# Issuing four key blocks first, reordering the tail of cross-attention, and making half of three layer norms one stage earlier

## The chip, the cores and the metric

The kernel runs on one core of one Trainium2 chip. The metric is device time in microseconds (us) of that core; lower is better. The engines are TensorE (PE, its weight loads PEld), VectorE (DVE), ScalarE (ACT), GpSimd (POOL) and SyncE (SP), which issues most of the DMAs. Each engine works through its own instructions in order and waits only on semaphores.

## The reference

The input x has 8 batches of 128 rows of 128 numbers, and a context of 8 x 77 rows of 96. Two decoder layers are computed, each of three sublayers that add to x. All four norms taken ahead of a sublayer subtract a row's mean and divide by its deviation:

```
layer 0: x += attention(norm(x))          16 heads of 64, with a relative position bias
         x += cross_attention(norm(x), context)   16 heads of 8, 77 keys
         x += mixture(norm(x))            16 experts, 8 chosen by sigmoid scores, and a shared one
layer 1: x  = strided attention block(norm(x)), with its own post-norms and a feed-forward part
         x += cross_attention(norm(x), context)
         x += mixture(norm(x))            8 experts of width 512, 2 chosen, with a capacity limit
```

## The kernel before

The kernel is one program in stages, each a block that all engines enter and leave together: setup (with norm 0), `attention0`, cross-attention of layer 0 (called x0 below), `mixture0`, `layer_norm("n3_")` (norm 2), `attention1`, cross-attention of layer 1 (x1), `mixture1`, store. Row vectors live on the 128 partitions, batches side by side: `x_all` and `xn_all` are [128, 8, 128], and `xnT_all` is the transposed copy that the matmuls read.

A norm of all eight batches (`norm_vector`, `norm_gpsimd`, `norm_tensor`, `norm_scalar`) is: on DVE four `bn_stats`, four `bn_aggr` and one add of epsilon (L173, L176, L178) for batches 0 to 3, the same for 4 to 7, then eight `tensor_scalar` (L181) that write the normed rows; on POOL one power for each half (L188); on PE eight transposes (L193); on ACT one copy for each half (L198). Norm 1 stands at the beginning of x0, norm 2 in a block of its own between `mixture0` and `attention1`, norm 3 at the beginning of x1. Norms ahead of the two mixtures are made inside cross-attention, batch by batch (L1021 to L1072).

**Cross-attention** (`cross_attention(l, ...)`) begins with its norm. Then PE makes the queries of batches 0 and 1 for all head groups (L821), ACT and DVE split them into a high and a low part (L923, L980), and the queries of batches 2 to 7 (L826, L935, L988) are brought to their place by DMA: SP issues 12 copies for part j = 0 (batches 2, 3) and 12 for part 1 (L807). The keys of a batch are one DMA of 462 KB into one of four buffers (L797). Before, SP issues the keys of batches 0 and 1, then part 0 of the queries, then keys of batches 2 and 3, then part 1, then in x1 six loads for the next stage, and then the keys of batches 4 to 7. The main loop has 16 steps n (two for each batch) of a software pipeline: scores of step n (PE L867), clamp and maximum (DVE L1008 and L1025; in x1 L1011 and L1029), subtraction (POOL L1063 in x0), exponential (ACT L968), transposes (PE L901), copy (ACT L963), values (PE L891), and for each batch the turn back (PE L911), the division (DVE L1040, L1044), transposes (PE L874), the output product (PE L857), the addition to x (DVE L1016), and the norm for the mixture: statistics on DVE, power and rows on POOL (L1068, L1071), transpose (PE L880), copy (ACT L946), router logits (PE L1145 or L1805). Steps 16 to 24 drain this pipeline. Within one step DVE adds to x first (batch (n-7)/2) and divides last (batch (n-5)/2). PE waits in step 4 for part 0 of the queries and the keys of batch 2, in step 8 for part 1 and the keys of batch 4.

**mixture0** has 34 units u: the shared expert on both halves of the rows, then experts 0 to 15 on the first half (u = 2 to 17), then on the second (u = 18 to 33). In step u PE makes gate(u) and up(u) (L1209 to L1211), and down(u-3). ACT takes the silu (L1287), POOL multiplies by the routing weight (`e_gc`, L1304), DVE multiplies by up (`e_h`, L1342), ACT copies the high part (L1266), DVE subtracts (`e_h_lo`, L1348). After step 22 the first half is turned back on PE (L1243) and DVE adds it to x (L1354) after its unit 22.

## Time and profile before

| | us |
|---|---|
| median of 3 runs | 558.77 |
| lowest, highest | 557.69, 562.34 |
| the profiled execution, its own time | 559.68 |
| its span in the trace | 557.9 |
| PE, DVE, ACT, POOL busy | 474.1, 371.1, 332.8, 267.3 |

The span is the time from the first to the last instruction of the profiled execution; its own time is 1.78 longer. Busy shares are means over stages with different limits, so for a change that touches stage borders the timeline around each border has to be read: which instruction starts late, and what released it. PEclk is TensorE's granted clock as a share of 2.4 GHz; 0.50 is 1.2 GHz.

### The profile page before, as it was taken

To read this page: it belongs to the slowest core of one execution; us is meant where nothing else is said; L and a number is where in the kernel's file an instruction comes from. 1 tells how busy PE (TensorE), PEld (TensorE's weight loads), DVE (VectorE), ACT (ScalarE), POOL (GpSimd) and SP (SyncE) were. 2 spreads that over 40 slices of the span, in tenths; PEclk is the share of its full clock that TensorE was granted. 3 is DMA by queue.
4 is the path that set the end of the run, shared out by engine and by line. 5 is a ranking of instruction groups with operands and counts; after the bars stand their busy time and mean duration, and the time that the engine had idled before them with its cause. 6 is when DMAs were issued, how large, how long until landed. Compare 5 with 4: busy or idle time off the path is not lost. (4 is left out here: it accounts for less than half of the span.)

```text
span 557.9 us, 9954 instructions
## 1 busy us (share of the span) xinstructions
PE 474.1 (85%) x3161; PEld 359.8 (64%) x3161; DVE 371.1 (67%) x911; ACT 332.8 (60%) x655; POOL 267.3 (48%) x294
## 2 busy tenths in 40 slices
PE   4689999999578877899994999656689779999995
PEld 3577888876356655688882578444466556777774
DVE  4787777774646745566665476767357454999995
ACT  3687777775446763356552465224467555988883
POOL 1699879777434642466662750113072231745420
PEclk9799999999779995899997899796789969999999
DMA  6614342425255000444332200003580002111101
GB/s 184 210 43 120 101 120 72 126 79 133 71 140 147 1 2 1 136 133 132 116 93 69 58 0 1 0 1 78 139 218 1 2 2 75 33 45 38 38 0 38
DMA packets 34688, 41.80 MB, mean 75 GB/s; under 512 B 5178, under 2 KB 26612, under 8 KB 34420
## 3 DMA queue, kind: packets, MB, share of 16 engines
q1 hardware_dynamic: 33796, 40.65, 26.2%
q10 hardware_dynamic: 848, 0.60, 0.4%
q8 instruction: 23, 0.38, 0.3%
q14 instruction: 21, 0.17, 0.1%
HBM read 30.70 MB, written 8.18 MB: 70 GB/s over the span
## 5 line engine op out<-in xcount | busy, mean ns | idle before, releaser
L1304 POOL TENSOR_TENSOR e_gc<-e_g,e_c 128x512 f32<-128x512 f32 x32 | 41.8, 1309 | 38.1 <-ACT e_g L1287 23.1
L2090 DVE TENSOR_TENSOR e_h_lo<-e_h,e_h_hi 128x512 fp32r<-128x512 f32 x56 | 55.6, 1045 | 3.4 <-ACT e_h_hi L1968 3.4
L1780 POOL TENSOR_TENSOR m_w_hi<-m_w,m_one 128x512 fp32r<-128x512 f32 x16 | 19.7, 1232 | 68.1 <-DMA m_w<-in_L_ffn_W 30.4
L963 ACT ACTIVATE x_pT<-x_turn 77x1024 f32<-77x1024 f32 x32 | 32.7, 1021 | 32.3 <-PE x_turn L901 32.3
L1964 ACT ACTIVATE e_h<-e_h,m_b 128x512 f32<-128x512 f32 x64 | 43.8, 691 | 8.3 <-PE e_h L1864 8.3
L557 ACT ACTIVATE a_p<-xn_all,a_least 128x128 f32<-128x128 f32 x128 | 40.7, 390 | 6.1 <-DVE a_least L596 6.0
L1266 ACT ACTIVATE e_h_hi<-e_h 128x512 fp32r<-128x512 f32 x34 | 21.5, 632 | 33.8 <-DVE e_h L1342 23.9
L901 PE MATMUL x_turn<-consts,x_p 128*77 128x128 f32 x256 | 38.3, 296 | 3.9 <-ACT x_p L968 3.9
L1348 DVE TENSOR_TENSOR e_h_lo<-e_h,e_h_hi 128x512 fp32r<-128x512 f32 x34 | 23.7, 698 | 26.5 <-ACT e_h_hi L1266 26.5
L703 POOL TENSOR_TENSOR a_p<-a_p,a_r 128x512 f32<-128x512 f32 x32 | 33.3, 1042 | 15.0 <-DVE a_r L605 15.0
L901 PEld LDWEIGHTS x_turn<-consts,x_p 128*77 128x77 f32 x256 | 30.3, 158 | 13.4 <-ACT x_p L968 11.1
L593 DVE TENSOR_TENSOR xn_all<-a_score,w_bias 128x256 f32<-128x256 f32 x64 | 24.1, 418 | 18.6 <-PE a_score L446 18.6
L1968 ACT ACTIVATE e_h_hi<-e_h 128x512 fp32r<-128x512 f32 x56 | 33.9, 636 | 0.0
L1063 POOL TENSOR_TENSOR x_s<-x_s,x_m 128x616 f32<-128x616 f32 x16 | 19.5, 1217 | 27.7 <-DVE x_m L1025 27.7
L891 PE MATMUL x_pv<-x_pT,vx 77*9 77x128 f32 x512 | 22.5, 299 | 9.6 <-ACT x_pT L963 9.6
L547 ACT ACTIVATE a_pT<-a_turn 128x512 f32<-128x512 f32 x32 | 19.0, 593 | 19.4 <-PE a_turn L456 19.4
L1862 PE MATMUL e_h<-m_x_hi,m_w_hi 128*128 128x512 f32 x64 | 26.4, 412 | 0.0
L1011 DVE TENSOR_REDUCE x_m<-x_score 128x8 f32<-128x616 f32 x16 | 12.7, 794 | 20.3 <-PE x_score L867 20.2
L867 PE MATMUL x_score<-x_ks,x_qs 96*128 96x308 f32 x64 | 19.2, 386 | 7.7 <-DMA x_ks<-kstack 6.4
L1864 PE MATMUL e_h<-m_x_hi,m_w_lo 128*128 128x512 f32 x64 | 25.6, 400 | 0.0
L1863 PE MATMUL e_h<-m_x_lo,m_w_hi 128*128 128x512 f32 x64 | 25.6, 400 | 0.0
L1862 PE MATMUL e_y<-e_h_hi,m_w_hi 128*128 128x512 f32 x56 | 24.9, 444 | 0.4 <-DVE e_h_lo L2090 0.4
(300 smaller groups left out, 1448.2 us busy)
## 6 DMA issues: line engine op xcount, KB each, us to landing
e_c<-spread SPq DMA_DIRECT2D x32, 256.0 KB, 3.3
x_ks<-kstack SPq DMA_DIRECT2D x16, 462.0 KB, 5.5
kstack<-a_blk_hi SPq DMA_DIRECT2D x32, 154.0 KB, 3.1
m_w<-in_L_ffn_W SPq DMA_DIRECT2D x16, 256.0 KB, 3.1
a_raw<-in_experts SPq DMA_DIRECT2D x17, 192.0 KB, 2.5
kstack<-a_blk_lo SPq DMA_DIRECT2D x16, 154.0 KB, 2.9
su_reversed<-scratch SPq DMA_DIRECT2D x1, 1024.0 KB, 5.6
w_wkv<-in_L_attn_Wkv SPq DMA_DIRECT2D x1, 1024.0 KB, 7.6
```

The source lines that it names most:

```text
L557: act.activation(p[n % 4][:, h, :], s[n % 2][:, h, :], ACT.Exp, bias=least[:, n % 4, h:h + 1]).then_inc(S["exp_done"], 1)
L593: dve.tensor_tensor(s[n % 2][:, own_heads, :], score[half][:, 0:2, :], bias0[:, NG * hg + half:NG * hg + NG:2, :], ALU.add).then_inc(S["bi ...
L703: pool.tensor_tensor(p[n % 4][:, :, :], p[n % 4][:, :, :], free(r[:, n % 4, :], [[1, NG], [0, P]]), ALU.mult).then_inc(S["normed"], 1)
L901: mm = pe.transpose(tb[0:NKV, u, P * j:P * j + P], p[k % 2][:, u, j, :], ident)
L963: act.activation(pT[k % 2][:, :, :], tb[0:NKV, :, :], ACT.Copy).then_inc(S["turned_out"], 1)
L1304: pool.tensor_tensor(gc[k % 2][:, :], g[u % 2][:, :], c[k % NC][:, :], ALU.mult).then_inc(S["weighted"], 1)
L1862: pe.matmul(out, w_hi, hi, start=start, stop=False)
L1863: pe.matmul(out, w_hi, lo, start=False, stop=False)
L1864: return pe.matmul(out, w_lo, hi, start=False, stop=stop)
L1964: act.activation(h[half][f], hb[f][:, :], ACT.Gelu, bias=b1[j][:, f:f + 1]).then_inc(S["gelu_done"], 1)
L1968: act.activation(h_hi[half][f - 1][:, :], h[half][f - 1], ACT.Copy).then_inc(S["hi_done"], 1)
L2090: dve.tensor_tensor(h_lo[half][f][:, :], h[half][f], h_hi[half][f][:, :].bitcast(F32), ALU.subtract).then_inc(S["lo_done"], 1)
```

## The change

`norm_vector` and `norm_gpsimd` are cut into functions for one half h: `norm_stats`, `norm_rows`, `norm_power`. Then:

- Norm 1, batches 0 to 3: statistics in `attention0` after DVE's step n = G = 32, the power after POOL's last step, the rows after DVE's step 35. x0 keeps batches 4 to 7.
- Norm 2, batches 0 to 3: in `mixture0`, statistics after DVE's unit 23, power after POOL's unit 24, rows after DVE's unit 25, four transposes after PE's step 27 (into the bank `rb`), ACT's copy after its step 28. The later turn of the second half waits for that copy.
- Norm 3, batches 0 to 3: statistics between the two halves of the last norm in `attention1`, the power on POOL after its third; the rows are the first work of DVE in x1.
- Cross-attention, both layers: SP issues the keys of batches 0 to 3 first. In the drain (n > 16) DVE divides before it adds to x; the rows of batch 7 are written by DVE instead of POOL; the router logits are issued in steps 17, 19, 21, 23 and 24 instead of 18, 20, 22 and 24.

The setup block calls the same functions in the same order as before.

```diff
-    def norm_vector(dve, n):
-
-        for h in range(2):
-            half = slice(HB * h, HB * h + HB)
-            for b in range(HB * h, HB * h + HB):
-                dve.bn_stats(stats[:, b, :], x_all[:, b, :]).then_inc(stats_done, 1)
-            for b in range(HB * h, HB * h + HB):
-                dve.wait_ge(stats_done, B * n + b + 1)
-                dve.bn_aggr(mv[:, b, :], stats[:, b, :]).then_inc(mv_done, 1)
-            dve.wait_ge(mv_done, (B + 2) * n + (HB + 1) * h + HB)
-            dve.tensor_scalar(var[:, half], mv[:, half, 1], LN_EPS, None, ALU.add).then_inc(mv_done, 1)
-        for b in range(B):
-            dve.wait_ge(rstd_done, 2 * n + b // HB + 1)
+    def norm_stats(dve, n, h):
+        half = slice(HB * h, HB * h + HB)
+        for b in range(HB * h, HB * h + HB):
+            dve.bn_stats(stats[:, b, :], x_all[:, b, :]).then_inc(stats_done, 1)
+        for b in range(HB * h, HB * h + HB):
+            dve.wait_ge(stats_done, B * n + b + 1)
+            dve.bn_aggr(mv[:, b, :], stats[:, b, :]).then_inc(mv_done, 1)
+        dve.wait_ge(mv_done, (B + 2) * n + (HB + 1) * h + HB)
+        dve.tensor_scalar(var[:, half], mv[:, half, 1], LN_EPS, None, ALU.add).then_inc(mv_done, 1)
+
+    def norm_rows(dve, n, h):
+        dve.wait_ge(rstd_done, 2 * n + h + 1)
+        for b in range(HB * h, HB * h + HB):
             dve.tensor_scalar(xn_all[:, b, :], x_all[:, b, :], mv[:, b, 0:1], rstd[:, b:b + 1],
                               ALU.subtract, ALU.mult).then_inc(normed, 1)
 
-    def norm_gpsimd(pool, n):
-        for h in range(2):
-            half = slice(HB * h, HB * h + HB)
-            pool.wait_ge(mv_done, (B + 2) * n + (HB + 1) * (h + 1))
-            pool.tensor_tensor(rstd[:, half], var[:, half], eps_pow[:, half], ALU.pow).then_inc(rstd_done, 1)
+    def norm_power(pool, n, h):
+        half = slice(HB * h, HB * h + HB)
+        pool.wait_ge(mv_done, (B + 2) * n + (HB + 1) * (h + 1))
+        pool.tensor_tensor(rstd[:, half], var[:, half], eps_pow[:, half], ALU.pow).then_inc(rstd_done, 1)
...
-                norm_vector(dve, n)
+                norm_stats(dve, n, 1)
+                norm_rows(dve, n, 1)
 
             @block.gpsimd
             def _(pool):
-                norm_gpsimd(pool, n)
+                norm_power(pool, n, 1)
 
             @block.tensor
             def _(pe):
-                norm_tensor(pe, n, turned)
+                norm_tensor(pe, n, turned, half=1)
 
             @block.scalar
             def _(act):
-                norm_scalar(act, n, turned)
+                norm_scalar(act, n, turned, half=1)
...
+                    if n == G:
+                        dve.wait_ge(S["x_out"], 2)
+                        norm_stats(dve, 1, 0)
+                    if n == G + 3:
+                        norm_rows(dve, 1, 0)
...
+                norm_power(pool, 1, 0)
...
-                keys(0)
-                keys(1)
+                for b in range(KEYS):
+                    keys(b)
...
-                    if j == 0:
-                        for b in range(2, KEYS):
-                            keys(b)
...
-                    if ahead is not None and n >= STEPS + 2 and n % 2 == 0:
-                        for b in range(0 if n == STEPS + 2 else n // 2 - 5, n // 2 - 4):
+                    if ahead is not None and (n > STEPS and n % 2 == 1 or n == 2 * SLOTS + 4):
+                        for b in {STEPS + 1: (0, 1), STEPS + 3: (2, 3, 4), 2 * SLOTS + 4: (7,)}.get(n, (n // 2 - 5,)):
                             pe.wait_ge(S["xT_out"], since["xT_out"] + b + 1)
                             ahead.logits(pe, b, tb)
...
-                norm_vector(dve, norm)
+                if l == 1:
+                    norm_rows(dve, norm, 0)
+                norm_stats(dve, norm, 1)
+                norm_rows(dve, norm, 1)
...
+                def finish(b):
+                    dve.wait_ge(S["back_done"], since["back_done"] + b + 1)
+                    dve.reciprocal(r[:, :], back[:, :, DH]).then_inc(S["recip_done"], 1)
+                    dve.wait_ge(S["recip_done"], since["recip_done"] + b + 1)
+                    if b >= 2:
+                        dve.wait_ge(S["slot_done"], since["slot_done"] + b - 1)
+                    dve.tensor_tensor(o[b % 2][:, :].rearrange("p (h d) -> p h d", d=DH), back[:, :, 0:DH],
+                                      free(r[:, 0:1], [[1, H], [0, DH]]), ALU.mult).then_inc(S["normed"], 1)
...
+                    if n > STEPS and batch_at(n, 5) is not None:
+                        finish(batch_at(n, 5))
...
+                    if b == B - 1:
+                        dve.wait_ge(S["rstd_done"], since["rstd_done"] + B)
+                        dve.tensor_scalar(xn_all[:, b, :], x_all[:, b, :], mv[:, b, 0:1], rstd[:, b:b + 1],
+                                          ALU.subtract, ALU.mult).then_inc(S["xn_done"], 1)
+                    if n < STEPS and batch_at(n, 5) is not None:
+                        finish(batch_at(n, 5))
...
-                norm_gpsimd(pool, norm)
+                norm_power(pool, norm, 1)
...
+                    if b is not None and b < B - 1:
...
+    NEXT = 2
...
+    ADDED = LAST_OF[0] + LAG + 2
...
-                    pe.wait_ge(S["added"], 1)
+                    pe.wait_ge(copied, 2 * NEXT + 1)
...
+                if u == ADDED + 5:
+                    norm_tensor(pe, NEXT, [rb[:, :]], half=0)
...
+                if u == ADDED + 6:
+                    norm_scalar(act, NEXT, [rb[:, :]], half=0)
...
+                if u == ADDED + 2:
+                    norm_power(pool, NEXT, 0)
...
+                if u == ADDED + 1:
+                    dve.wait_ge(S["added"], 1)
+                    norm_stats(dve, NEXT, 0)
+                if u == ADDED + 3:
+                    norm_rows(dve, NEXT, 0)
...
+                    if k == 2:
+                        norm_power(pool, 3, 0)
...
+                    if h == 0:
+                        dve.wait_ge(S["x_ready"], HB)
+                        norm_stats(dve, 3, 0)
```

## Rows read from the trace of the kernel before

**Rows 1.** Windows: PE, PEld, DVE, ACT, POOL busy (instructions), clock, DMA share, GB/s.

```profile
140.90:215.80 74.90, 56.29 (x516) 40.89 (x516) 42.59 (x115) 42.43 (x68) 34.96 (x35) 0.83 0.26 67
216.50:298.60 82.10, 77.31 (x318) 60.99 (x318) 49.97 (x106) 43.19 (x74) 41.85 (x32) 0.95 0.34 104
```

**Rows 2.** Timeline, beginning of x0: start, us, engine line, tiles, [idle before <-releaser].

```profile
140.94 1.28 ACT L920 ACT_TABLE_LOAD   x1 [1.24 <-PEq L327]
...
140.97 0.87 DVE L173 BATCH_NORM_STATS2 stats<-x_all 128x6 f32<-128x128 f32 x4 [0.32 <-PEq L327]
...
142.40 1.02 POOL L188 TENSOR_TENSOR rstd<-var,eps_pow 128x4 f32<-128x4 f32 x1 [5.27 <-DVE var L178]
...
143.49 2.36 DVE L181 TENSOR_SCALAR xn_all<-x_all,mv,rstd 128x128 f32<-128x128 f32 x8
...
145.16 0.60 ACT L198 ACTIVATE xnT_all<-x_turn 128x512 f32<-128x512 f32 x1 [2.93 <-PE x_turn L193]
```

**Rows 3.** Window over attention0's last 8 us, columns as in rows 1.

```profile
132.20:140.20 8.00, 6.95 (x49) 4.42 (x47) 1.27 (x3) 2.23 (x5) 4.77 (x6) 1.00 0.34 80
```

**Rows 4.** Timeline, DVE in the last microseconds of attention1.

```profile
371.14 0.69 DVE L1729 TENSOR_TENSOR a_y<-b_pv,xn_all 128x512 f32<-128x512 f32 x1 [2.73 <-PE b_pv L1556]
```

**Rows 5.** Timeline, beginning of x1.

```profile
376.04 0.87 DVE L173 BATCH_NORM_STATS2 stats<-x_all 128x6 f32<-128x128 f32 x4 [0.32 <-PEq L1440]
...
380.24 0.60 ACT L198 ACTIVATE xnT_all<-x_turn 128x512 f32<-128x512 f32 x1 [2.94 <-PE x_turn L193]
...
382.60 0.48 DVE L980 SCALAR_TENSOR_TENSOR x_qs<-x_score,cols,x_qs 32x256 fp32r<-32x256 f32 x1 [1.68 <-ACT x_qs L923]
```

**Rows 6.** Timeline, keys issued by SP and the score products that waited for them.

```profile
159.16 1.05 SPq L797 DMA_DIRECT2D x_ks<-kstack  x2
...
163.63 0.85 PE L867 MATMUL x_score<-x_ks,x_qs 96*128 96x308 f32 x2 [0.70 <-DMA x_ks<-kstack]
...
395.12 1.05 SPq L797 DMA_DIRECT2D x_ks<-kstack  x2
...
399.48 0.85 PE L867 MATMUL x_score<-x_ks,x_qs 96*128 96x308 f32 x2 [3.96 <-DMA x_ks<-kstack]
...
413.94 0.52 PE L867 MATMUL x_score<-x_ks,x_qs 96*128 96x308 f32 x2 [1.72 <-DMA x_ks<-kstack]
```

**Rows 7.** Timeline, the drain of x0.

```profile
205.98 0.63 PE L911 MATMUL x_back<-consts,x_oS 128*128 128x128 f32 x4 [0.78 <-ACT xnT_all L946]
...
208.47 0.25 DVE L1040 RECIPROCAL x_r<-x_back 128x16 f32<-128x16 f32 x1
...
213.36 0.80 POOL L1071 TENSOR_SCALAR xn_all<-x_all,mv,rstd 128x128 f32<-128x128 f32 x1
...
214.31 0.45 PE L880 MATMUL x_back<-consts,xn_all 128*128 128x128 f32 x1 [1.17 <-POOL xn_all L1071]
```

**Rows 8.** Timeline, mixture0's loop: DVE's units 24 and 25, PE's step 28.

```profile
276.42 0.68 DVE L1342 TENSOR_TENSOR e_h<-e_up,e_gc 128x512 f32<-128x512 f32 x1
...
278.41 0.68 DVE L1342 TENSOR_TENSOR e_h<-e_up,e_gc 128x512 f32<-128x512 f32 x1
...
279.79 0.69 DVE L1348 TENSOR_TENSOR e_h_lo<-e_h,e_h_hi 128x512 fp32r<-128x512 f32 x1 [0.70 <-ACT e_h_hi L1266]
...
280.70 0.40 PE L1209 MATMUL e_gate<-e_x_hi,we_hi 128*128 128x512 f32 x1
```

**Rows 9.** Timeline of POOL, mixture0's loop: the product in two places.

```profile
234.48 1.47 POOL L1304 TENSOR_TENSOR e_gc<-e_g,e_c 128x512 f32<-128x512 f32 x1 [0.23 <-ACT e_g L1287]
...
276.34 1.33 POOL L1304 TENSOR_TENSOR e_gc<-e_g,e_c 128x512 f32<-128x512 f32 x1 [1.17 <-ACT e_g L1287]
```

**Rows 10.** Windows in mixture0 and x0, columns as in rows 1.

```profile
160.00:170.00 10.00, 9.30 (x74) 6.76 (x75) 3.57 (x5) 4.58 (x7) 2.43 (x2) 0.50 0.84 200
...
225.00:227.00 2.00, 0.00 (x0) 0.00 (x0) 1.79 (x15) 0.00 (x0) 0.00 (x0) 1.00 0.09 25
228.00:231.00 3.00, 3.00 (x8) 2.35 (x8) 0.43 (x1) 0.00 (x0) 1.84 (x2) 0.50 0.81 282
```

More of the change, by code:

```diff
@@ L307, in _ @@
                 dve.wait_ge(ld_x, 16)
-                norm_vector(dve, 0)
+                for h in range(2):
+                    norm_stats(dve, 0, h)
+                for h in range(2):
+                    norm_rows(dve, 0, h)
                 dve.wait_ge(ld_bias, 16)
@@ L315, in _ @@
                 pool.wait_ge(eps_set, 1)
-                norm_gpsimd(pool, 0)
+                for h in range(2):
+                    norm_power(pool, 0, h)
         return mine
@@ L1036, in _ @@
                                           ALU.add).then_inc(S["var_done"], 1)
-                    b = batch_at(n, 5)
-                    if b is not None:
-                        dve.wait_ge(S["back_done"], since["back_done"] + b + 1)
-                        dve.reciprocal(r[:, :], back[:, :, DH]).then_inc(S["recip_done"], 1)
-                        dve.wait_ge(S["recip_done"], since["recip_done"] + b + 1)
-                        if b >= 2:
-                            dve.wait_ge(S["slot_done"], since["slot_done"] + b - 1)
-                        dve.tensor_tensor(o[b % 2][:, :].rearrange("p (h d) -> p h d", d=DH), back[:, :, 0:DH],
-                                          free(r[:, 0:1], [[1, H], [0, DH]]), ALU.mult).then_inc(S["normed"], 1)
+                    if b == B - 1:
[4 more added lines that the diff above has]
+                        finish(batch_at(n, 5))
                     if ahead is not None and n == 2 * B + 4:
@@ L1093, in program @@
         mixture0(nc, tools, spread0, x_all, xnT_all, consts, tables, we_hi, we_lo, we_split,
-                 lambda ahead: cross_attention(0, past_sems=past_sems, ahead=ahead))
-        attention1(nc, a, tools, layer_norm, x_all, xn_all, xnT_all, consts, rows, cols, eps_pow, pick)
+                 lambda ahead: cross_attention(0, past_sems=past_sems, ahead=ahead),
+                 (norm_stats, norm_rows, norm_power, norm_tensor, norm_scalar, copied))
+        attention1(nc, a, tools, layer_norm, x_all, xn_all, xnT_all, consts, rows, cols, eps_pow, pick,
+                   norm_stats, norm_power)
         mixture1(nc, a, tools, cross_attention, x_all, xn_all, xnT_all, consts, tables)
@@ L1113, in split_weights, with mixture0 @@
             left = rest[:, :, 0:experts]
-def mixture0(nc, tools, spread, x_all, xnT_all, consts, tables, w_hi, w_lo, w_split, cross_attention):
+def mixture0(nc, tools, spread, x_all, xnT_all, consts, tables, w_hi, w_lo, w_split, cross_attention, norm):
     ident = consts[:, 0:P]
@@ L1121, in mixture0 @@
     HB = B // 2
+    norm_stats, norm_rows, norm_power, norm_tensor, norm_scalar, copied = norm
+    NEXT = 2
     SHARED = E0
@@ L1364, in _, with attention1 @@
                     add_out(0)
+                if u == ADDED + 1:
[3 more added lines that the diff above has]
+                    norm_rows(dve, NEXT, 0)
             add_out(1)
-def attention1(nc, a, tools, layer_norm, x_all, xn_all, xnT_all, consts, rows, cols, eps_pow, pick):
+def attention1(nc, a, tools, layer_norm, x_all, xn_all, xnT_all, consts, rows, cols, eps_pow, pick, norm_stats, norm_power):
     bout, b2, gamma, beta = (rows[:, k, :] for k in (2, 3, 4, 5))
```

## The prediction

> **What bounds the kernel.** I read the busy table, then windows over whole stages, then the timeline around each place that the change touches. The windows show two kinds of stage. In x0 PE is busy 56.29 of 74.90 us, at a mean granted clock of 0.83: no engine is full, and a latency chain sets the time. In mixture0 PE is busy 77.31 of 82.10 us: PE sets the time, and whatever holds it up is lost [rows 1]. So work taken off the chain in x0, x1 or a norm counts in full; work put into mixture0 counts if PE must wait for it. Times below are starts unless said otherwise.
>
> **Beginning of x0.** DVE makes statistics of both halves from 140.97 and rows from 143.49, so one half's statistics take 2.52 / 2 = 1.26 us; eight rows take 2.36, four 1.2; ACT's first copy is at 145.16 [rows 2]. After the change the rows of batches 0 to 3 are there when the stage begins. PE turns them by about 142.0, but ACT loads its table until 142.22, so its copy is at 142.3: 2.85 earlier. The second half follows in time: DVE's statistics to 142.2, POOL's power (1.02) to 143.4, rows to 144.7 [rows 2], while PE and ACT make the first queries, which takes them about as long. Gain 2.8. What was moved lies in attention0's last 8 us, where DVE is busy 1.27 and POOL 4.77 [rows 3]: 1.26 of statistics, 1.02 of power and 1.2 of rows fit into the 6.7 and 3.2 us left. They cost nothing; without that cover they would cost up to 3.5.
>
> **Beginning of x1.** Statistics go into the 2.73 us in which DVE waits before 371.14 [rows 4] and cost nothing. The rows of the first half stay in x1: done by 376.04 + 1.2 = 377.25, beside ACT's table load. ACT's copy, before at 380.24, comes at 377.7. But DVE then makes the other half's statistics (to 378.5), waits for the power (to 379.7) and makes rows to 380.95, so its first split of the queries, 382.60 before, comes at 380.95 at best [rows 5]. Gain 1.7.
>
> **Norm 2.** One half's statistics less on the chain: 1.25 [rows 2].
>
> **Keys first.** In x0 the keys of batches 2 and 3 are issued at 159.16, behind 12 query copies, and PE waits 0.70 us for them before 163.63; it had work of its own until 162.93. In x1, issued at 395.12, they hold PE for 3.96 us before 399.48 [rows 6]. Issued at the stage's beginning, they are there long before step 4. So x0 gains 0.7. In x1 the next wait takes over: at 413.94 PE waits 1.72 for the keys of batch 4 [rows 6], which stand on SP behind part 1 of the queries and six weight loads. SP has 1.05 us less to issue ahead of them, and I put 0.4 on query copies no longer slowed by key blocks under way: these keys come 1.45 earlier, not 3.96. A longer pause of PE before them leaves it at the lower clock afterwards, which I put at 0.35. So x1 gains 1.1. Bounds: nothing in either, and in x0 2.6 more, if PE's 10 us at a granted clock of 0.50 after 160 [rows 10] are mostly gone.
>
> **Drain of x0 and x1.** The division of batch 7 waits behind the addition of batch 6 and comes at 208.47, though PE began to turn that batch at 205.98, for 0.63 [rows 7]. Dividing first makes it about 1.8 earlier, but PE's logits, now in steps 17 and 19, stand ahead of both pairs of transposes and take back some. I carry 1.6 to the last addition to x. The rows of batch 7 take POOL 0.80 at 213.36 [rows 7]; DVE needs 2.36 / 8 = 0.3 [rows 2]: 0.5 more. So PE's last transpose, at 214.31 [rows 7], comes 2.1 earlier. x1 runs through the same list: 1.9. Bounds: half of both, with the logits in the way, and 0.2 more than either.
>
> **mixture0, the cost.** Before, DVE starts e_h of units 24 and 25 at 276.42 and 278.41, e_h_lo of unit 25 at 279.79, and PE its step 28 at 280.70 [rows 8]. Now:
> - DVE's four statistics, means and the addition come first: e_h(24) at 276.42 + 1.26 = 277.68, and e_h(25) could follow at 278.41 + 1.26 = 279.67;
> - POOL's power stands behind e_gc(24) in its queue and waits for these statistics: 276.42 + 1.43 (142.40 - 140.97 in [rows 2]) = 277.85, ending at 278.9. Behind it waits e_gc(25), at 276.34 before [rows 9]: now at 279.0, and with 1.33 us it ends at 280.3;
> - that product now lies wholly beside DVE's e_h_lo(24). At 234.48, partly beside one, it took 1.47 us instead of 1.33 [rows 9]; wholly, I take 0.3: 280.6;
> - e_h(25) at 280.65, e_h_lo(25) 1.38 later (279.79 - 278.41) at 282.05, the rows 0.6 after that at 282.65, four of them done at 283.85;
> - PE reaches its four transposes at 280.70 and must wait for those rows: step 28 begins at about 284.15. Loss 3.45.
>
> PE's pause has a second price. From 225 to 227 PE stands, and from 228 to 231 it is granted 0.50, 1.2 GHz, while fully busy [rows 10]: 3 us at half speed lose 1.5 of work, and here PE is the bound. I take 1.6; the ends are nothing, and 5, which 10 us at 0.50 as after 160 [rows 10] would lose.
>
> A page of the Trainium skill speaks against this placing too: GPSIMD Engine Reference, in the opening table, has GpSimd's interfaces to SBUF shared with VectorE, and names contention with VectorE instructions in a 2-port mode or with two SBUF inputs. The slower product at 234.48 agrees in kind [rows 9]. If by that rule each engine waited out the other's whole e_h_lo or product, 0.7 us [rows 8] would stand in place of my 0.3, and the kernel would be 0.4 later.
>
> **Sum.** -2.8 (x0 begins) - 0.7 (keys) - 2.1 (drain) + 3.45 + 1.6 (mixture0) - 1.25 (norm 2) - 1.7 (x1 begins) - 1.1 (keys) - 1.9 (drain) = -6.5. The profiled execution took 559.68; it is 0.9 over the median of 558.77, and against the median the sum gives 552.3. A measurement of this kernel tells about 1%, 5.6 us, from no change; "faster" begins below 553.2.
>
> **Rivals.**
> 1. *The clock stays up.* PE waits in mixture0 but is not slowed after it, and in x0 the slow 10 us mostly go. For it: in the pause at 225 to 227 the granted clock was still 1.00, so what a pause does depends on where it falls. Against: a pause of 3.45 is longer than that one, which had its price [rows 10]. 552.3 - 1.6 - 2.6 = 548.1. Chance 0.16.
> 2. *Later waits take the gains of chains.* The first keys are late with four blocks under way: two blocks in flight released PE 4.4 us after issue [rows 6], four sharing evenly would take 8.8, against the 5 that x0 leaves; I price 1.9. The drains give half (2.0 less), x1's keys nothing (1.1 less). 552.3 + 5.0 = 557.3. For it: 413.94 shows one such wait already [rows 6]. Against: blocks issued in order should land in order. Chance 0.25.
> 3. *Slower.* After PE's pause the lower clock stays for the rest of mixture0's loop. Six units of 2 us (the distance of two e_h [rows 8]) are left, 12 us of PE work, which take 24: 552.3 - 1.6 + 12 = 562.7. The kernel becomes slower than before once PE does over 8 of these 12 us of work at half clock. For it: the 10 us at 0.50 after 160. Against: after 228 the full clock came back in about 3 us to a PE as busy as in this loop [rows 10]. Chance 0.07.
> 4. *The moved halves bring nothing*, because the stages wait for their second half anyway: the gains of 2.8, 1.25 and 1.7 fall away, and 552.3 + 5.75 = 558.1 is left. Against: the second rows would be done at 144.7, when PE comes to them [rows 2]. Chance 0.06.
>
> **How the numbers follow.** The forecast's own case has 0.46, and the predicted time is its 552.3. The range takes rival 1 and nearly all of rival 2: 547.5 to 557.5; rivals 3 and 4 and the edges of the others are left out. Faster by over 1%: rival 1 and nearly all of the forecast's case, less a few hundredths for its upper half: 0.57. Slower by over 1% than 558.77 needs the far end of rival 3 and is nearly empty; with what I may have overlooked, 0.06. Within 1%: 0.37.
>
> **What would show it.** Right: ACT's first copy in x0 directly after its table load; in mixture0 PE idle some 3 us before four transposes of xn_all, and a granted clock of 0.50 behind them; in x1 no wait for keys in step 4 and a longer one in step 8; the last transpose of x0's drain 5.6 earlier (2.8 + 0.7 + 2.1). Wrong: PE not waiting in mixture0, or over 5 us; step 0 of a cross-attention waiting for its keys; POOL's power in mixture0 with nothing queued late behind it.

## The result and the profile after

| us | before | after |
|---|---|---|
| median of the runs | 560.84 (20 runs) | 556.92 (20 runs) |
| lowest, highest | 557.69, 564.91 | 554.36, 560.05 |
| profiled execution: own time, span | 559.68, 557.9 | 557.54, 555.8 |

The ratio is 0.9926, 95% interval 0.9905 to 0.9946: 0.7% faster, some 4 us, where 6.5 were forecast. 556.92 lies in the range, but the change falls within 1% and not beyond it. The forecast time of 552.3 was counted from a median of 558.77 over three runs; over 20 runs the kernel before takes 560.84, so the forecast time lies 8.5 below it, of which only 6.5 was forecast gain. The two profiled executions differ by 2.1 us only. So the first question is where 6.5 us became 2.1, the second why the medians show 3.9.

**Stages.** A stage runs here from its first load or instruction to the next one's. Both columns are read from the timelines.

| stage, us | before | after | difference | forecast |
|---|---|---|---|---|
| setup, attention0 | 140.95 | 140.37 | -0.58 | 0 |
| x0 | 75.58 | 70.22 | -5.36 | -5.6 |
| mixture0 | 83.73 | 89.35 | +5.62 | +5.05 |
| norm 2, to attention1's first product | 6.40 | 6.11 | -0.29 | -1.25 |
| attention1 behind that product | 69.34 | 71.35 | +2.01 | 0 |
| x1 | 76.88 | 71.99 | -4.89 | -4.7 |
| mixture1 | 105.02 | 106.41 | +1.39 | 0 |

x0, mixture0 and x1 came out at the forecast lengths, within 0.6; for x0 and x1 that is luck, since errors of opposite sign meet there, as the experiments show. The rest of the loss stands in the norm 2, attention1 and mixture1 rows. Each column is one execution, and the same code varies: see "What was chance" below.

Windows of the kernel after, over x0 and mixture0 (columns as in rows 1):

```profile
140.40:209.80 69.40, 55.05 (x516) 41.02 (x516) 40.99 (x102) 42.45 (x68) 33.06 (x33) 0.85 0.28 73
210.60:298.30 87.70, 79.56 (x324) 61.45 (x325) 54.14 (x119) 43.20 (x75) 43.26 (x33) 0.95 0.33 97
```

Against [rows 1], PE's busy time in x0 is nearly the same and the stage 5.4 shorter: its waits went. In mixture0 the stage grew by 5.6 and PE's busy time by 2.25 of that: four transposes more, and several products at 1.2 GHz.

The beginnings of x0 and x1, and the last transpose of x0's drain:

```profile
140.36 1.28 ACT L927 ACT_TABLE_LOAD   x1 [1.24 <-PEq L331]
141.66 0.60 ACT L197 ACTIVATE xnT_all<-x_turn 128x512 f32<-128x512 f32 x1
...
379.14 0.60 ACT L197 ACTIVATE xnT_all<-x_turn 128x512 f32<-128x512 f32 x1 [0.44 <-PE x_turn L192]
...
202.99 0.26 DVE L1004 RECIPROCAL x_r<-x_back 128x16 f32<-128x16 f32 x1 [1.86 <-PE x_back L918]
...
208.38 0.45 PE L887 MATMUL x_back<-consts,xn_all 128*128 128x128 f32 x1 [0.40 <-DVE xn_all L1060]
```

ACT's copy in x0 comes 1.30 after the stage's first row, where it came 4.22 after in [rows 2]: 2.9 earlier, right behind its table load. The last transpose comes 68.0 after that row, against 73.4 [rows 2, 7].

mixture0, the four engines around the moved pieces:

```profile
270.64 0.86 DVE L171 BATCH_NORM_STATS2 stats<-x_all 128x6 f32<-128x128 f32 x4
...
271.93 0.69 DVE L1372 TENSOR_TENSOR e_h<-e_up,e_gc 128x512 f32<-128x512 f32 x1
273.32 1.57 DVE L1378 TENSOR_TENSOR e_h_lo<-e_h,e_h_hi 128x512 fp32r<-128x512 f32 x1 [0.70 <-ACT e_h_hi L1292]
274.81 0.68 DVE L1372 TENSOR_TENSOR e_h<-e_up,e_gc 128x512 f32<-128x512 f32 x1
276.19 0.69 DVE L1378 TENSOR_TENSOR e_h_lo<-e_h,e_h_hi 128x512 fp32r<-128x512 f32 x1 [0.70 <-ACT e_h_hi L1292]
276.80 2.06 DVE L181 TENSOR_SCALAR xn_all<-x_all,mv,rstd 128x128 f32<-128x128 f32 x4
...
272.07 1.02 POOL L187 TENSOR_TENSOR rstd<-var,eps_pow 128x4 f32<-128x4 f32 x1 [2.68 <-DVE var L176]
273.05 2.98 POOL L1332 TENSOR_TENSOR e_gc<-e_g,e_c 128x512 f32<-128x512 f32 x2
276.72 1.28 POOL L1332 TENSOR_TENSOR e_gc<-e_g,e_c 128x512 f32<-128x512 f32 x1 [0.68 <-ACT e_g L1313]
...
278.14 1.24 PE L192 MATMUL e_route<-consts,xn_all 128*128 128x128 f32 x4 [2.22 <-DVE xn_all L181]
279.04 0.78 PE L1233 MATMUL e_gate<-e_x_hi,we_hi 128*128 128x512 f32 x1
```

The power, `e_gc` and `e_h_lo` meet here, and each instruction by itself is:

```profile
273.05 1.29 POOL L1332 TENSOR_TENSOR e_gc<-e_g,e_c 128x512 f32<-128x512 f32 x1
...
274.30 1.73 POOL L1332 TENSOR_TENSOR e_gc<-e_g,e_c 128x512 f32<-128x512 f32 x1
```

Mixture0 now begins 5.94 earlier. With 5.94 added, e_h(24) stands at 277.87 (forecast 277.68), the power at 278.01 (277.85), e_h(25) at 280.75 (280.65), its low part at 282.13 (282.05). The rows begin at 282.74 (282.65) as forecast, but take 2.06 instead of 1.2, and step 28 begins at 284.98 (284.15). The loss is 4.28 instead of 3.45. That e_h(25) hit its time is luck: the forecast had it wait for a POOL product slowed by 0.3, but that product took 1.29, and what ended late was DVE's own e_h_lo(24), which began 0.27 behind the product and took 1.57 instead of 0.69. The next product, begun 0.59 before e_h_lo's end, took 1.73. The e_gate behind the transposes takes 0.78 instead of 0.40: 1.2 GHz, as forecast.

Between mixture0 and attention1, and x1's step 8:

```profile
302.48 1.12 DVE L181 TENSOR_SCALAR xn_all<-x_all,mv,rstd 128x128 f32<-128x128 f32 x4 [1.13 <-POOL rstd L187]
...
302.88 1.25 PE L192 MATMUL n_turned<-consts,xn_all 128*128 128x128 f32 x4 [3.93 <-DVE xn_all L181]
306.05 6.65 PE L1510 MATMUL b_score<-xnT_all,a_wqkv 128*128 128x512 f32 x8 [1.92 <-DMA a_w<-in_L_attn_W]
...
395.60 0.55 PE L874 MATMUL x_score<-x_ks,x_qs 96*128 96x308 f32 x2 [1.10 <-DMA x_qs<-x_q_lo]
...
411.29 0.85 PE L874 MATMUL x_score<-x_ks,x_qs 96*128 96x308 f32 x2 [5.12 <-DMA x_ks<-kstack]
```

The shorter norm 2 uncovered a load: attention1's first product waits until all five of its weight loads have landed. And in x1 the wait of step 4 for keys is gone, as forecast; the one of step 8 grew from 1.72 [rows 6] to 5.12.

### The profile page after: what moved, and what is told of

It reads as the page before. It is cut to its first block and busy times, and to the rows that moved or that the text cites. A ratio compares the mean times of both kernels' runs of the same rounds, so it can differ in the third digit from the quotient of the medians.

```text
span 555.8 us, 9954 instructions
## 1 busy us (share of the span) xinstructions
PE 474.1 (85%) x3161; PEld 358.3 (64%) x3161; DVE 373.8 (67%) x913; ACT 332.3 (60%) x655; POOL 265.3 (48%) x292
## 5 line engine op out<-in xcount | busy, mean ns | idle before, releaser
L1081 POOL TENSOR_TENSOR x_s<-x_s,x_m 128x616 f32<-128x616 f32 x16 | 19.5, 1216 | 25.7 <-DVE x_m L1046 25.7
L898 PE MATMUL x_pv<-x_pT,vx 77*9 77x128 f32 x512 | 21.2, 287 | 10.6 <-ACT x_pT L970 10.6
L1904 PE MATMUL e_h<-m_x_hi,m_w_lo 128*128 128x512 f32 x64 | 26.1, 407 | 0.0
L417 PE MATMUL a_fill<-a_x_hi,a_w_hi 128*128 128x256 f32 x64 | 20.0, 313 | 6.7 <-ACT a_w_hi L536 5.9
```

What stands on the lines that cost most here:

```text
L1904: return pe.matmul(out, w_lo, hi, start=False, stop=stop)
```

## The experiments

Each ratio is taken to the kernel before on the same chip; lengths are of the one profiled execution. "The changed kernel" is the one after. "Norm to x1" is the stretch from norm 2's block to the start of x1. "Without it" means kernels that leave norm 2 whole behind mixture0; their mixture0 takes 83.71 to 84.81 us in seven executions, 83.9 in the mean.

**e1_no_norm2.** `norm_tensor(pe, NEXT, ...)`, its copy, power, statistics and rows are taken out of mixture0, and the block between does both halves again.

> The changed kernel without its move into mixture0: norm 2 stands whole in the block between mixture0 and attention1 again; keys, drain and norms 1 and 3 stay changed. Theory A (the move costs its 5.6 us inside mixture0, and its 1.26 us at the block between come back as a wait for the last of attention1's weight loads and as a longer stretch at 1.2 GHz at attention1's start): mixture0 83.8 us instead of 89.4, the stretch from norm 2 to x1 shorter than the 77.45 of the changed kernel, at 75.7 as before; 6.5 us under the changed kernel, near 550.4. Rival B (the longer attention1 is the chance of one profiled execution, the 1.26 is gained for good): 5.6 less 1.26 = 4.3 us under it, near 552.6, and attention1 with its norm 77 or so. Rival C (mixture0's added length is not the moved pieces but where the clock falls in it after an earlier start): within 1 us of the changed kernel, mixture0 again 89.

Measured: 552.46, ratio 0.986 (0.983 to 0.9889). mixture0 84.81, norm to x1 76.00. That is 8.2 us under before, where the changed kernel is 3.9 under it: the move costs 4.3 by the medians, 3.7 by the ratios. The size is Rival B's, though 76.00 is A's length; the table of attention1 under "What was chance" shows why that one length decides nothing.

**e2_only_norm2.** The reverse: the kernel before with this move alone.

> The kernel before with the move into mixture0 alone. Theory A: mixture0 +5.6, nothing back behind it, so 5.5 to 6.5 us slower than the kernel before, near 567. Rival B: +5.6 - 1.26 = 4.3 slower, near 565. Rival C: same as before within 1 us. In both A and B the products of the first and second moved steps show a POOL product of 1.5 us and a VectorE subtraction of 1.57 beside it.

Measured: 568.03 (seven runs, 562.04 to 569.39), ratio 1.013 (1.0101 to 1.0159), 7.4 slower. The profiled execution was the fastest of the seven: mixture0 88.12 (+4.4), norm to x1 74.80 (-0.9). The sign is shown, the size is not: 7.4 here, 3.7 to 4.3 in e1. The profiled execution had the shortest mixture0 and the shortest attention1 (69.10) of all kernels with this move in this place; others took up to 91.34 and 73.29, together 7.4 more. That could be the 3.7 to 7.4 us which the other six took more, but no trace of those six is there to show it.

**after_again.** The changed kernel unchanged, under another name.

> The changed kernel itself once more, for the length of its stages in a second execution. If the longer attention1 (77.45 us with the norm ahead of it, against 75.7 before) and the longer start of mixture1 belong to the change, they come again within 0.3 us; if they are where the clock happens to rise in one execution, attention1 with its norm comes out between 74.8 and 77.5. mixture0 by both 88 to 89.5.

Measured: 558.6, ratio 0.9933 (0.9906 to 0.9959), the same as at first. mixture0 89.32, x0 69.68, x1 72.67: the same. Attention1 behind its first product took 73.20, though, not 71.35; with its norm 78.83, longer than either reading expected.

**e3_norm2_spread.**

```
-                if u == ADDED + 1:
-                    dve.wait_ge(S["added"], 1)
-                    norm_stats(dve, NEXT, 0)
-                if u == ADDED + 3:
-                    norm_rows(dve, NEXT, 0)
+                if ADDED + 1 <= u <= ADDED + 4:
+                    b = u - ADDED - 1
...
+                    norm_stats(dve, NEXT, 0, (b,))
+                if ADDED + 7 <= u <= ADDED + 10:
+                    norm_rows(dve, NEXT, 0, (u - ADDED - 7,))
```

The last argument names the batches. The power stands three units later, PE's transposes seven and ACT's copy six.

> The changed kernel with the same moved instructions of norm 2 spread out in mixture0: one batch's statistics with each of four units, the power with the fifth, one batch's rows with each of units 7 to 10, TensorE's four transposes and ScalarE's copy behind the last gate. Theory A' (the loss in mixture0 is that 1.3 and 1.1 us blocks of VectorE and the power in front of a POOL product make the three engines' chain late by more than its slack, and that the transposes wait in TensorE's queue for the late rows): 4 to 5 us of the 5.6 come back, mixture0 84.5 to 85.5, time 552 to 553. Rival D (the loss is the added work itself, wherever it stands, since POOL and VectorE disturb each other in every unit): under 1.5 us comes back. TensorE's clock stays at 2.4 GHz through the loop by A', and drops again by D.

Measured: 559.98, ratio 0.9989 (0.9966 to 1.0013), mixture0 91.20: worse than the change, against both theories, until its rows are read. (By the ratios it is worse beyond their intervals. By mixture0's length alone it would not be shown, since e6 below took 91.34 with the changed kernel's mixture0.) The timeline of DVE, then of POOL:

```profile
285.53 1.32 DVE L183 TENSOR_SCALAR xn_all<-x_all,mv,rstd 128x128 f32<-128x128 f32 x1
288.76 1.31 DVE L183 TENSOR_SCALAR xn_all<-x_all,mv,rstd 128x128 f32<-128x128 f32 x1
291.97 1.30 DVE L183 TENSOR_SCALAR xn_all<-x_all,mv,rstd 128x128 f32<-128x128 f32 x1
295.17 0.34 DVE L183 TENSOR_SCALAR xn_all<-x_all,mv,rstd 128x128 f32<-128x128 f32 x1
...
285.45 1.31 POOL L1334 TENSOR_TENSOR e_gc<-e_g,e_c 128x512 f32<-128x512 f32 x1 [0.68 <-ACT e_g L1315]
288.68 1.30 POOL L1334 TENSOR_TENSOR e_gc<-e_g,e_c 128x512 f32<-128x512 f32 x1 [1.91 <-ACT e_g L1315]
```

Three rows began 0.08 us behind a POOL product and ended 0.09 behind its end (the first at 286.85 and 286.76); the fourth, with no product beside it, took 0.34. A row is held for as long as the product lasts. Spread out, four rows meet three products and lose 1.0 each; in one block, as in the changed kernel, they meet one, and the other three follow 0.26 apart: 2.06 = 1.28 + 3 x 0.26. The Trainium skill, Trainium Architecture — The Big Picture, "What this means for kernel authors", calls what VectorE and GpSimd share "an exclusive lock (not a bandwidth split)"; these rows agree. Statistics beside a product were not held (in this run 0.29 at 270.75, with a product from 270.67). The clock stayed at 1.00 from 272 to 290, as the first theory had it.

**e5_gap.** In each unit DVE idles 0.70 between e_h and e_h_lo, waiting for ACT's high half, and POOL has then just finished.

```
                 values(u)
+                if u in (ADDED + 1, ADDED + 2):
...
+                    k = 2 * (u - ADDED - 1)
+                    norm_stats(dve, NEXT, 0, (k, k + 1))
+                if u in (ADDED + 5, ADDED + 6):
+                    k = 2 * (u - ADDED - 5)
+                    norm_rows(dve, NEXT, 0, (k, k + 1))
                 low_part(u)
...
-                if u == ADDED + 2:
+                if u == ADDED + 4:
                     norm_power(pool, NEXT, 0)
```

PE's transposes and ACT's copy stand three units later, two behind the last rows.

> The changed kernel with norm 2's moved instructions put where VectorE waits for ScalarE's high half anyway, between the product and the low part of a unit (statistics of two batches in each of the first two units, rows of two batches in each of the fifth and sixth), the power behind the fourth unit's POOL product, TensorE's transposes two units behind the rows. Theory F (a row on VectorE that meets a POOL product is held until that product ends, 1.3 us instead of 0.3, as in the spread version; in the gap POOL has just finished): rows 0.3 us each, no TensorE wait over 0.5 us, mixture0 84.5 to 85.5, so 4 us under the changed kernel: 552 to 553. Rival D (the added work itself disturbs): mixture0 over 87.

Measured: 552.82, ratio 0.9841 (0.9816 to 0.9867), mixture0 84.25. The same instructions, 5 us cheaper. Two of the rows on DVE, then PE's transposes:

```profile
279.20 0.98 DVE L183 TENSOR_SCALAR xn_all<-x_all,mv,rstd 128x128 f32<-128x128 f32 x2
...
283.18 0.60 PE L194 MATMUL e_route<-consts,xn_all 128*128 128x128 f32 x4
```

Two rows take 0.98, a remnant of the hold (the product of 278.52 ends at 279.84), and no engine waits for it; the transposes take 0.60 at 2.4 GHz without a wait before them, where they took 1.24 behind 2.22 of waiting.

**e12_rows_gap** and **e13_stats_gap**: one of these two places alone.

> The changed kernel with only the rows of norm 2 moved into VectorE's gap (two batches each, in the third and fourth unit), transposes and copy one unit later; statistics and power as in the changed kernel. Theory F1 (the rows' block, 2.06 us with the wait for POOL's product in it, just after a block of statistics that had eaten the slack, makes the transposes' wait of 2.2 us and the clock's drop behind it): mixture0 86 to 87, no drop. Rival F2 (the statistics and the power are the larger part): over 88.

> The changed kernel with the statistics of norm 2 in VectorE's gap and the power one unit after them, the rows in one block behind the low part of the fifth unit. F1: the rows' block alone, 2.1 us on a chain that has its full slack, costs 1 us or less of wait: mixture0 84.5 to 86. F2: the same or lower, 84.5. If the rows' block alone is enough for the loss: over 87.

Measured: 553.07 (ratio 0.9838, 0.9792 to 0.9884), mixture0 86.52; and 553.85 (0.9861, 0.9815 to 0.9908), mixture0 86.48. Either alone takes back 2.8 to 2.9 of the 5.1 that both take back. Read the other way: statistics and power left in their old place cost 2.6 over the 83.9 without it, the rows' block left in its place 2.6, and both together 4.2 to 7.4 in six executions. The losses add. F1's length holds for the first, but its reason, a slack that the statistics had eaten, does not: with all slack left, the rows' block was to cost 1 us or less and cost 2.6. By the ratios, on four runs each, either alone is already as good as both (0.9838 and 0.9861, against 0.9841), so the split within mixture0 rests on single profiles.

**e4_qkv_wait.**

```
-            sp.dma_start(wqkv[:, :], a["L1_attn_Wqkv"]).then_inc(ld, 16)
+            sp.dma_start(wqkv[:, :], a["L1_attn_Wqkv"]).then_inc(ld_qkv, 16)
-                pe.wait_ge(ld, 80)
+                pe.wait_ge(ld_qkv, 16)
...
+                pe.wait_ge(ld, 64)
```

The second wait stands ahead of the products with the select matrices.

> The changed kernel with a semaphore of its own for attention1's first weight load, so that its first products don't wait for all five loads. Theory A (the 1.92 us idle before these products is the last load): they start 1.0 us earlier, at 305.0 instead of 306.05 by the changed kernel's profile, and the time is 0.5 to 1.5 us less. Rival E (the wait only gives the place: the clock rises at the same moment after the start of the products and the select matrices' wait takes the gain): 0 to 0.3 us.

Measured: 554.02, ratio 0.988 (0.9853 to 0.9907). From norm 2's block to attention1's first product 5.12, against 6.11 and, over nine executions with the five-load wait, 5.62 to 6.11. The full 1.28 is there only without that wait. By the ratios the kernel gains 2.6 us on the changed one; that is more than this wait and isn't explained by it.

**e8_only_keys, e9_only_drain, e10_only_norms13.** The kernel before with one of the other parts each.

> The kernel before with only the order of the key loads changed. By the prediction's terms 0.7 in x0 and 1.1 in x1, 1.8 us less. Rival I (x1's middle is bound by the weight splits on POOL, which end 9.3 us after the weights land and stand ahead of norm 3's first power in POOL's queue; keys that land earlier change nothing behind that): x0 0.5 to 1 shorter, x1 within 0.3 of its 76.85, 0.7 us less in all.

> The kernel before with only the drain's order changed (reciprocal and product ahead of the other work, the last row on VectorE, the logits' places). By the prediction 2.1 in x0 and 1.9 in x1, 4.0 us less. Rival J (the drain is worth half, since its last stretch runs at 1.2 GHz): 2 us.

> The kernel before with only the halves of norms 1 and 3 moved ahead. By the prediction the start 2.8 in x0 and 1.7 in x1 earlier, 4.5 us less. Rival I: in x1 the start's 1.7 us is swallowed where step 8 waits for keys whose load is set by SP's queue (the x_qs loads start 1.7 earlier too, so only a part), 3.5 us less.

| us | ratio to before | x0 | x1 |
|---|---|---|---|
| before | 1 | 75.58 | 76.88 |
| keys | 0.9993 (0.9966 to 1.002) | 76.53 | 77.09 |
| drain | 0.9951 (0.9926 to 0.9977) | 73.05 | 75.58 |
| norms 1 and 3 | 0.9902 (0.9865 to 0.9939) | 71.82 | 73.15 |

The three add up to the stages of the changed kernel: -5.3 in x0 (75.58 to 70.22: -5.4), -4.8 in x1 (-4.9). But keys first brought no gain in either (+1.0 and +0.2, where -0.7 and -1.1 were forecast), and the two halves of the norms 7.5, not 4.5. By the ratios the drain brings 2.8, between the forecast 4.0 and Rival J's 2, and the norms 5.5, more than the 4.5 and Rival I's 3.5. The interval of the keys' ratio alone, 1.9 us less to 1.1 more, would just admit the 1.8; the stages of this one execution show nothing of it. In x0 with the keys alone PE's 0.70 wait is gone, but the stage has 29.3 us at a granted clock of 0.50, where it had 26.1. In x1 with the keys alone:

```profile
414.68 0.85 PE L871 MATMUL x_score<-x_ks,x_qs 96*128 96x308 f32 x2 [5.69 <-DMA x_ks<-kstack]
```

Step 4 comes 3.0 earlier in the stage (20.48 after its start, not 23.48), step 8 1.2 earlier (36.74, not 37.94), behind a wait of 5.69, after which PE is at 1.2 GHz, so that step 9 is 0.3 later than before (41.63, 41.36).

**e6_keys4.** The keys of batches 4 and 5 are issued ahead of mixture1's weight loads; nothing else differs from the changed kernel.

> The changed kernel with the keys of batches 4 and 5 issued ahead of mixture1's weight loads in x1. Theory G (the 5.12 us wait of the products of step 8 is for keys 4, whose load stands behind six weight loads in SP's queue, and only their place is late): the wait goes, x1 67.5 to 69 instead of 71.9, 3 to 4.5 us less. Rival H (the same bytes land no sooner, or the next wait, for the keys of batch 6 or of the first splits of mixture1, takes it): under 1.5 us less.

**e14_splits_only.** POOL's four splits of these weights stand behind the rows of batches 0 to 3, one each, instead of all ahead of the first power.

> The changed kernel with the weight splits in x1 spread out behind the rows of batches 0 to 3, the keys of batches 4 and 5 still behind the weight loads. Theory L (two waits end within a microsecond of each other in x1's middle, for keys 4 and for POOL's first row behind the splits; taking away one leaves the other): the 5.1 us wait for keys stays and x1 is 70.5 to 72. Rival M (the splits alone were the bound, and the wait for keys hides nothing): x1 67 to 68.5.

**e7_best.** No norm 2 in mixture0, keys 4 early, attention1's own semaphore.

> The changed kernel without the move into mixture0, with the keys of batches 4 and 5 ahead of the weight loads and a semaphore of its own for attention1's first weights. The last is worth little here, since the whole norm stands ahead of attention1 again (its products began 0.94 us after the copies, not at a load): 0 to 0.3. Sum by theories A and G: 4.3 + 4 = 8 us under the changed kernel, 548 to 550. By rival H 552.

Measured: keys 4 early 560.67, ratio 0.9974 (0.9947 to 1.0), x1 75.81, 3.8 longer than in the changed kernel (and mixture0, with unchanged code, 91.34). Splits spread 557.13, ratio 0.9921 (0.9894 to 0.9949), x1 72.33. e7_best 556.3, ratio 0.9903 (0.9882 to 0.9925), x1 75.79: of the 3.7 to 4.3 us that e1 gained on the changed kernel, 1.3 to 1.8 are left. Theory G fails: its wait goes, its gain does not come. PE in x1 with keys 4 early, and POOL:

```profile
407.53 0.52 PE L874 MATMUL x_score<-x_ks,x_qs 96*128 96x308 f32 x2 [1.02 <-DMA x_ks<-kstack]
...
422.26 0.48 PE L887 MATMUL x_back<-consts,xn_all 128*128 128x128 f32 x1 [8.96 <-POOL xn_all L1090]
...
419.52 1.26 POOL L1822 TENSOR_TENSOR m_w_lo<-m_w,m_w_hi 128x512 fp32r<-128x512 f32 x1
420.74 0.56 POOL L1086 TENSOR_TENSOR rstd<-var,eps_pow 128x1 f32<-128x1 f32 x1
421.41 0.80 POOL L1090 TENSOR_SCALAR xn_all<-x_all,mv,rstd 128x128 f32<-128x128 f32 x1
```

The keys' wait shrank to 1.02, and PE stood 8.96 for POOL's first row, behind 9.4 us of splits that began later, 33.0 into the stage instead of 30.0, as the weights now landed later. With the splits spread and the keys late:

```profile
409.90 0.85 PE L874 MATMUL x_score<-x_ks,x_qs 96*128 96x308 f32 x2 [6.58 <-DMA x_ks<-kstack]
```

Theory L holds (72.33 lies 0.3 above its range): two waits over the same microseconds; take away one, and the other is left. That taking away both shortens the stage is shown next.

**e11_best2**: the gap, keys 4 early, splits spread and attention1's own semaphore together. **e15_best_no2**: the same with norm 2 whole behind mixture0.

> The gap version of norm 2, the keys of batches 4 and 5 ahead of the weight loads, attention1's first weights on a semaphore of their own, and the splits of mixture1's first weights on POOL one by one behind the rows of batches 0 to 3 instead of all four ahead of the first power. Theory I (in the keys-4 version TensorE's 8.96 us wait for POOL's first row was these splits in front of it, and that is what took the 4 us that the keys gave): x1 67 to 68.5 instead of 72 to 75.8; time 547 to 549.5 against 560 to 562 of before. Rival K (POOL's splits disturb VectorE wherever they stand, or are late for mixture1's start): x1 over 70 or mixture1 over 107, time 551 or more.

> The best version so far without any of norm 2 in mixture0. If the moved half is worth its 1.28 us at the block between less 0.6 of TensorE in mixture0: 0.3 to 1 us slower than the best version's 546.6 of that call, and its lengths are mixture0 83.8 and 6.4 from norm to attention1. If it is worth nothing: the same within 0.5.

Measured: 546.63, ratio 0.9751 (0.9711 to 0.9791), x1 65.07; and 546.65, ratio 0.9718 (0.9678 to 0.9757), x1 66.23. Some 15 us under before. All waits of PE in x1 over 0.7 us, in the first of them:

```profile
PE x_turn L194 <- DVE xn_all L183: 5.3, 1, 5.3
PE x_pv L900 <- ACT x_pT L972: 4.9, 14, 0.8
PE x_score L876 <- DVE x_qs L992: 0.9, 2, 0.5
PE x_score L876 <- DMA x_ks<-kstack: 0.8, 1, 0.8
```

(Columns: us in total, times, the longest.) The two medians agree, and the intervals of the ratios overlap: even placed well, the half norm in mixture0 brings nothing that can be measured.

**What was chance.** In attention1 the change adds only statistics and a power, which lie in a wait of DVE (it still waits 1.35 behind them). Its length from its first product on, in 18 executions:

| us | attention1 behind its first product |
|---|---|
| norm 2 whole (7) | 69.34, 69.46, 69.60, 71.37, 71.81, 71.84, 71.85 |
| half of it in mixture0 (11) | 69.10, 69.32, 69.36, 69.62, 69.78, 69.98, 71.21, 71.35, 71.87, 73.20, 73.29 |

The means are 70.75 and 70.73. What goes along with the length is the clock: the executions of 69.1 to 70.0 us spend 11.1 to 12.0 us of the stage at a granted clock of 0.50, those of 71.2 to 71.9 spend 13.3 to 17.3, those of 73.2 and 73.3 spend 18.6 and 18.7. The shortest (e2) and the long one of after_again, over the whole stretch:

```profile
309.16:378.26 69.10, 57.92 (x332) 42.15 (x332) 45.42 (x182) 29.05 (x68) 22.27 (x45) 0.92 0.05 12
```

```profile
305.70:378.90 73.20, 62.28 (x332) 45.28 (x332) 46.83 (x191) 29.25 (x68) 23.26 (x46) 0.87 0.05 11
```

The windows of its first 8 us, before and after, show PE's clock rise later in the second:

```profile
304.00:312.00 8.00, 7.06 (x16) 3.39 (x16) 2.58 (x7) 4.55 (x7) 2.22 (x7) 0.63 0.53 142
```

```profile
304.00:312.00 8.00, 6.08 (x8) 2.53 (x8) 1.47 (x3) 3.68 (x5) 2.76 (x7) 0.50 0.51 135
```

The profile of before had drawn the short kind, that of after the middle one: 2.0 us of the difference of the two profiles, none of that of the medians. Without it the profiles would differ by 4.1, and the medians do by 3.9. How close these are is itself chance, since other stages vary too: x0 takes 67.9 to 71.8 us in the 13 executions with all its parts changed.

mixture0 varies in the same way with the block in it. In e2, the changed kernel and e6 PE waits the same 2.22 before the four transposes. Ten microseconds of each of these three, in this order, from some 3 us before the first product behind the transposes (columns as in rows 1):

```profile
280.80:290.80 10.00, 8.06 (x35) 6.37 (x36) 7.25 (x12) 4.96 (x9) 5.22 (x4) 1.00 0.31 100
```

```profile
276.00:286.00 10.00, 7.86 (x29) 6.25 (x30) 6.56 (x12) 4.71 (x9) 3.97 (x5) 0.83 0.35 98
```

```profile
277.20:287.20 10.00, 8.04 (x25) 6.34 (x26) 5.85 (x10) 3.69 (x7) 3.63 (x3) 0.66 0.30 90
```

After the same pause the clock did not fall, fell for 3.4 us, and for 6.8 us, and mixture0 took 88.12, 89.35 and 91.34.

## Why the prediction was wrong, step by step

Two steps failed, "keys first" and "norm 2", and two terms were mis-sized, the drain and the rows in mixture0. By the ratios, which rest on many runs each (us of some 561; "in one" is e1, "norm 2's half" is the changed kernel less e1):

| gain, us | forecast | measured |
|---|---|---|
| keys first (e8) | 1.8 | 0.4 |
| drain (e9) | 4.0 | 2.8 |
| halves of norms 1 and 3 (e10) | 4.5 | 5.5 |
| these three in one (e1) | 10.3 | 7.9 |
| norm 2's half, in mixture0 | -3.8 | -3.7 |

The intervals reach 1.4 to 2.1 us to either side, so no single error is sure in size. The last two rows sum to the 4.2 us of the changed kernel's ratio, against 6.5 forecast: by this reckoning the shortfall stands in cross-attention, in the keys and the drain, and the norms gave more than forecast and hid a part of it. What norm 2's half costs is less settled: 3.7 here, 4.3 by the medians, 7.4 in e2, and 4.9 by the stages below, where both of its terms came out worse than forecast.

The stages show where. Means over all executions with the same arrangement take much of the chance out. Against the two to seven without it, those with the change show: x0 70.1 against 75.3 (-5.3), mixture0 89.4 against 83.9 (+5.5), norm to first product 5.76 against 6.40 (-0.6), attention1 0, x1 72.1 against 76.8 (-4.7), mixture1 105.9 against 105.3 (+0.6): -4.5. Setup with attention0 takes 141.1 with and without the moved half of norm 1, which so cost nothing, as forecast. The medians give -3.9 and, the second time, -3.4; the 0.6 to 1.1 between -4.5 and these is not explained.

- **Beginning of x0 and x1**: right as to the start (2.9 and 2.5 at ACT's copy; DVE's first split in x1 1.9 earlier in the stage, forecast 1.7). The stages gained more, 3.8 and 3.7, and the working has no term for it. It goes along with the clock: x0 spent 19.9 us at 0.50 instead of 26.1, x1 22.0 instead of 25.7. In x1 the wait for keys in step 4 stayed (4.06), the one in step 8 shrank from 1.72 to 1.33. Why the clock was higher is open.
- **Keys first, 1.8: failed.** No gain, ratio 0.9993. "SP has 1.05 us less to issue ahead of them" was right in kind (step 8 came 1.2 earlier, forecast 1.45); the price of a longer pause, "0.35", was not: it was 1.5 by step 9, behind a wait of 5.69 with PE at 1.2 GHz. In x0 the wait of 0.70 went, and 3.2 us more at 0.50 came. What the working did not see at all is that the weights' splits on POOL stand on a second path as long as that of the keys of batch 4, so that moving those keys too gains nothing by itself (e6, e14).
- **Drain, 4.0**: 3.8 in the two stages (2.5 and 1.3), right in sum, 0.6 short in x1. By the runs' ratio it is 2.8, by their medians 3.7. mixture1 is 0.6 longer in the changed kernel. Its first products take 0.63 each, and not 0.40, from 453.05 to 456.6 before and from 449.56 to 455.3 after: 3.6 us at 1.2 GHz became 5.7. This wasn't in the sum. It does not hang on the drain alone, since e10 with the old drain has 105.7 too.
- **mixture0, +5.05**: +5.5. The rows were mis-sized, 2.06 for 1.2, since only POOL's product was charged for the meeting and not DVE's own instructions. The times of e_h(25) and its low part came out by luck: the product beside e_h_lo was to lose 0.3 and lost nothing (1.29), and e_h_lo, to which the working gave no loss, lost 0.88. The clock's 1.6 came to 1.3 in this profile (5.62 less 4.28), to nothing in e2's and more in e6's.
- **Norm 2, 1.25: failed.** 0.6: the load behind it became the bound. It was not read what else attention1's first product waits for; with a semaphore of its own for that load the gain is 1.28 (e4).
- **The rivals**: the second was the nearest, 557.3, by later waits. Of its three parts the one on x1's keys came true; the first keys were not late, and the drains gave more than half. The first rival's missing clock drop in mixture0 did occur in one execution (e2), without its total. Nothing points to the third or fourth: the clock was back after 3.4 us, in e6 after 6.8, and the moved halves of norms 1 and 3 brought the most of all.

## What to carry to other kernels

Before moving work onto an engine that another one shares memory access with, lay both timelines side by side and put the piece where the other stands still: the same instructions cost 5.5 us in the mean, or 0.3 to 1.0, by place alone. When one wait is to be removed, list every path that ends within its length behind it, here the splits on POOL behind the keys and the fifth load behind the norm; each removal alone left x1 as long or made it 3.8 longer, both together made it 6 to 7 us shorter. Measure each part of a change alone: here the lengths of x0 and x1 came out right although the keys brought nothing, since the norms brought more. And of two profiles only stages that repeat over several executions may be compared: one stage drew 69.3, 71.4 or 73.2 us with the same code.

## What was not expected of the hardware

- A DVE tensor_scalar of 128x128 between SBUF tiles, started 0.08 behind a POOL product of 128x512, ended 0.09 behind its end, 1.32 instead of 0.34. A tensor_tensor of two SBUF tiles, started 0.27 behind such a product, ended 0.55 behind its end, 1.57 instead of 0.69, and the product queued next took 1.73 instead of 1.29. bn_stats (0.29) and POOL's power over four columns (1.01 beside a DVE low part of 0.69) were not disturbed.
- The same products can take longer by where the 1.2 GHz stretch lies: mixture1 took 105.0 to 105.3 us in the three executions with 3.7 to 3.9 us at 0.50 at its beginning, and 105.5 to 106.4 in the fifteen with 4.3 to 6.0.
- The same pause of PE, 2.22 us at the same place, was followed by no drop of the granted clock, by one of 3.4 us or by one of 6.8 us. Attention1's three lengths go along with its time at 0.50; why that time differs between executions stays open.
